# A decoder layer on one core: the setup reordered, constants and selecting columns moved

## The reference

```python
xx = shift(x, 1 token) - x                      # attention with decay, 32 heads of 8
r, k, v, g = (x + xx * maa_*) @ W*.T + b*;  g = silu(g)
w = exp(-exp(time_decay));  u = time_faaaa
Wm = where(i > j, w ** (i - j - 1), where(i == j, u, 0))     # per head
y = (r @ k * Wm) @ v + (state of earlier chunks)
y = (group_norm(y, 8 per head) * ln_g + ln_b) * g @ Wo.T + bo
# cross attention: 16 heads of 16, causal softmax over 128 keys from the context
# mixture: softmax router, 2 of 8 experts of width 176, a shared one of width 704 with a gate
```

## Time and profile before

| | |
|---|---|
| time, median of 3 | 620.1 us (619.21 to 621.57) |
| profiled execution | 619.4 us, span 617.7 us |
| TensorE busy | 591.4 us of the span (96%), 6488 instructions |
| VectorE, ScalarE, GpSimd busy | 404.3, 279.4, 335.0 us |
| TensorE's mean granted clock | 0.997 |
| setup: first instruction to first scores | 30.8 us |

### The profile page before, as it was taken

How to read it: one execution, slowest core, us unless ns; L and a number is a source line. 1 busy time by engine, 2 the same in 40 slices (tenths; PEclk the granted TensorE clock), 3 DMA queues, 4 the chain that set the end, 5 groups by cost and what they waited for, 6 DMA issues and landing times.

```text
span 617.7 us, 15901 instructions
## 1 busy us (share of the span) xinstructions
PE 591.4 (96%) x6488; PEld 479.7 (78%) x6488; DVE 404.3 (65%) x841; ACT 279.4 (45%) x637; POOL 335.0 (54%) x451
## 2 busy tenths in 40 slices
PE   7997898999999999999999999999999999999997
PEld 6544555645889999755889999864798999899997
DVE  5997896899745666879654666869762565752221
ACT  3876243222336566342335666251435656343332
POOL 7567110337446667614455766515364666619776
PEclk8999999999999999999999999999999999999999
DMA  8941000001121121011121112002021112115320
GB/s 192 341 128 36 0 2 2 2 19 54 37 77 35 46 65 45 14 29 59 28 84 30 43 55 59 21 18 71 14 54 38 41 45 61 31 52 126 88 56 18
DMA packets 41906, 34.18 MB, mean 55 GB/s; under 512 B 9917, under 2 KB 41286, under 8 KB 41834
## 3 DMA queue, kind: packets, MB, share of 16 engines
q1 hardware_dynamic: 39930, 31.34, 18.7%
q10 hardware_dynamic: 1904, 1.84, 0.9%
HBM read 30.98 MB, written 2.17 MB: 54 GB/s over the span
## 4 chain that ended last, share of the span: by engine, by line
PE 62%; DVE 19%; POOL 6%; issue 6%; ACT 5%; DMA 1%; ACTq 0%; POOLq 0%; DVEq 0%
DVE A L1630 8%; PE bank L1071 8%; PE bank L1072 7%; PE bank L1073 7%; PE bank L1067 7%; PE bank L1110 4%; PE bank L1111 4%; PE bank L1269 4%; PE bank L1113 3%; PE bank L1196 2%; PE bank L1064 2%; POOL hb L646 2%; PE bank L1350 2%; PE bank L1183 2%; PE bank L1320 2%
## 5 line engine op out<-in xcount | busy, mean ns | idle before, releaser
L633 POOL TENSOR_TENSOR hT<-hb,hT 128x256 fp32r<-128x256 f32 (+1 forms) x102 | 78.3, 768 | 71.7 <-ACT hT L816 71.7
L646 POOL TENSOR_TENSOR hb<-hb,cwb 128x256 f32<-128x256 f32 (+1 forms) x102 | 76.9, 754 | 53.3 <-DVE hb L1605 52.9
L1605 DVE TENSOR_TENSOR hb<-hb,bank 128x256 f32<-128x256 f32 (+1 forms) x102 | 42.7, 418 | 95.7 <-ACT hb L826 95.7
L816 ACT ACTIVATE hT<-hb 128x256 fp32r<-128x256 f32 (+1 forms) x102 | 42.4, 416 | 119.2 <-POOL hb L646 112.0
L1071 PE MATMUL bank<-xTf,wGh 128*128 128x256 f32 x272 | 82.5, 303 | 0.0
L1630 DVE TENSOR_TENSOR A<-bank,decay 128x512 f32<-128x512 f32 x128 | 77.3, 682 | 3.9 <-PE bank L1183 3.8
L1073 PE MATMUL bank<-xTf,wGl 128*128 128x256 f32 x272 | 75.9, 279 | 0.0
L1072 PE MATMUL bank<-xTf,wGh 128*128 128x256 f32 x272 | 75.9, 279 | 0.0
L1072 PE MATMUL bank<-xTf,wUh 128*128 128x256 f32 x256 | 71.5, 279 | 0.0
L1071 PE MATMUL bank<-xTf,wUh 128*128 128x256 f32 x256 | 71.5, 279 | 0.0
L1073 PE MATMUL bank<-xTf,wUl 128*128 128x256 f32 x256 | 71.3, 279 | 0.0
(11 more groups left out here) (235 smaller groups left out, 1405.8 us busy)
## 6 DMA issues: line engine op xcount, KB each, us to landing
cwb<-cw_rows SPq DMA_DIRECT2D x54, 128.0 KB, 2.9
A<-cw_rows SPq DMA_DIRECT2D x18, 128.0 KB, 4.0
A<-in_x SPq DMA_DIRECT2D x4, 512.0 KB, 4.4
res<-in_x SPq DMA_DIRECT2D x4, 512.0 KB, 4.3
out_x<-res SPq DMA_DIRECT2D x8, 256.0 KB, 2.7
rawG<-in_L_ffn_w_gate SPq DMA_DIRECT2D x2, 704.0 KB, 6.4
rawU<-in_L_ffn_w_up SPq DMA_DIRECT2D x2, 704.0 KB, 6.8
cwb<-cw_rows SPq DMA_DIRECT2D x12, 112.0 KB, 2.6
```

The costliest lines, as they stand in the source:

```text
L633: pool.tensor_tensor(low, hb[hr, c % 2, :], hT[hr, c % 2, 0, :].bitcast(F32), ALU.subtract).then_inc(h_lo, 1)
L646: pool.tensor_tensor(hb[hr, c % 2, :], hb[hr, c % 2, :], cwb[hr, c % CWS, :], ALU.mult).then_inc(h_scaled, 1)
L816: act.activation(hT[hidden(n), c % 2, 0, :], hb[hidden(n), c % 2, :], ACT.Copy).then_inc(h_hi, 1)
L1605: tt(h, h, up_part(PS[5 + c % 2], n), ALU.mult).then_inc(gu_used, 1)
```

## The change

Setup: VectorE takes the statistics of x ahead of `td_neg`. TensorE turns the norm ahead of the fourth weight, with no idle products ahead of it, and issues three idle products instead of five behind the weights. ScalarE takes the fourth weight after the first half of the turned norm, and `W_OUT` after r. Of the low 16 heads, VectorE adds the diagonal of the first eight; for heads 8 to 15 ScalarE writes diagonal matrices (`low_bonus_part`, eight instructions around the key copies) and GpSimd adds them at once (`low_diagonal`). `headsel` is written in two halves, one behind the second mixed input, one behind the eighth receptance, and `rev` behind that. The additions of the high diagonal come one receptance later.

Group 0: the seven score banks have another order, and the waits go with it (the gate is waited for by score product 6 in place of 3). `selecting_columns` moves behind `layer_rstd(1, g)`. Three of the four masking products of `key_scores` move into `turn_maxima`, in place of three idle products. `layer_apply(0, 1)` moves ahead of `attended(0)`.

```diff
         W_EARLY = 4
-        SCORE_BANKS = [0, 1, 3, 2, 5, 6, 7]
+
+        def score_bank(g, n):
+
+            return ([0, 1, 3, 2, 5, 6, 7] if g else [0, 1, 3, 5, 6, 7, 2])[n % 7]
...
                 made(pool.memset(onesp[:, w, XD * w:XD * w + XD], 1.0))
-            for n in range(E):
-                made(pool.memset(rev[:, n:n + 1], float(E - n)))
...
-            for b in range(GB):
+            def heads_of(b):
                 rows = headsel[32 * b:32 * b + 32]
...
                                             pattern=[[sign * P, KC], [sign, P]], channel_multiplier=-sign * N))
-            assert done[0] == CONSTS, done[0]
+
+            pool.wait_ge(xm_ready, 2)
+            heads_of(0)
+            heads_of(1)
...
+            def low_diagonal():
+                hs = slice(H // 4, H // 2)
+                pool.wait_ge(decay_cut, 1)
+                pool.wait_ge(low_bonus_made, 1)
+                pool.tensor_tensor(decay[:, hs, :], decay[:, hs, :], bonus[:, hs, :], ALU.add).then_inc(decay_half, 1)
+
             decay_cut_half(0)
...
             receptance(0, 1)
+            low_diagonal()
             decay_cut_half(1)
...
                         split_down(u)
-                    if g == 0 and u == 2:
+                    if g == 0 and u == 3:
                         diagonal(0)
-                    elif g == 0 and u == 3:
+                    elif g == 0 and u == 4:
                         diagonal(1)
...
                 if g == 0:
+                    pool.wait_ge(rbd_ready, 8)
+                    heads_of(2)
+                    heads_of(3)
+                    for n in range(E):
+                        made(pool.memset(rev[:, n:n + 1], float(E - n)))
+                    assert done[0] == CONSTS, done[0]
                     for n in range(3):
...
                     pool.wait_ge(xvp_rest, 2)
-                    selecting_columns()
                 point(g, "n1")
...
                 layer_rstd(1, g)
+                if g == 0:
+                    selecting_columns()
                 point(g, "n3")
...
-            def take_rk(g, key):
+            def take_rk(g, key, parts=range(2)):
                 if g == 0 and not key:
...
                     act.activation(rT[:, m, :], PS[r_bank(g, m)][:, :], ACT.Identity, bias=cols[:, BR, m:m + 1]).then_inc(r_ready, 1)
-                for m in range(2) if key else ():
+                for m in parts if key else ():
                     act.wait_ge(proj_done, g * 8 + 2 + m + 1)
...
             def bonus_half(n):
-                if n == 0:
-                    act.wait_ge(row_in, 16 * 8)
+                if n == 1:
+                    act.wait_ge(decay_half, 1)
                 for h in range(n * H // 4, (n + 1) * H // 4):
...
+            def low_bonus_part(n):
+                for h in range(n * H // 8, (n + 1) * H // 8):
+                    last = act.activation(bonus[:, h, :], ident[:], ACT.Copy, scale=tf[:, h:h + 1])
+                if n == 3:
+                    last.then_inc(low_bonus_made, 1)
+
             mixed_input(0)
+            take_weight(3, wA[:, 3])
             take_weight(W_O, wO[:])
             take_weight(W_Q, wQh[:])
-            take_weight(W_OUT, wX[:])
             decay_powers(0)
             take_rk(0, 0)
-            take_rk(0, 1)
+            take_weight(W_OUT, wX[:])
+            low_bonus_part(2)
+            take_rk(0, 1, (0,))
+            low_bonus_part(3)
+            take_rk(0, 1, (1,))
             decay_powers(1)
...
             idle_product(8, 7, True)
-            for n in range(W_EARLY):
+            for n in range(W_EARLY - 1):
                 turn_weight(n)
-            idle_product(5, 7, True)
             turn_norm(0, 0, tokx, 2)
-            for n in range(W_EARLY, W_KV):
+            for n in range(W_EARLY - 1, W_KV):
                 turn_weight(n)
-            idle_product(5, 4, True)
+            idle_product(3, 4, True)
             project(0, 0)
...
                     m, t = u // 4, slice((u % 4) * T, (u % 4 + 1) * T)
-                    if u == 0:
-                        if g == 0:
-                            pe.wait_ge(w_taken, taken_by_act(8))
+                    if u == 0 and g == 0:
+                        pe.wait_ge(w_taken, taken_by_act(W_OUT))
                     if u == 0 or u == 4:
...
                             pe.wait_ge(v_ready, g * 2 + 2)
-                        elif n == 3 and g != 1:
+                        elif n == 3 and g >= 2:
                             pe.wait_ge(g_ready, g * 2 + 2)
+                        elif n == 4 and g == 0:
+                            pe.wait_ge(w_taken, taken_by_act(W_KV))
+                        elif n == 5 and g == 0:
+                            pe.wait_ge(w_taken, taken_by_act(W_RT))
+                        elif n == 6 and g == 0:
+                            pe.wait_ge(g_ready, 2)
                         elif n == 4 and g >= 2:
...
                         rows = slice(32 * i, 32 * i + 32)
-                        mm(PS[SCORE_BANKS[n % 7]][:, :], kT[rows, m, t], rbd[rows, u % 2, :, :], start=True, stop=True).then_inc(s_ready, 1)
+                        mm(PS[score_bank(g, n)][:, :], kT[rows, m, t], rbd[rows, u % 2, :, :], start=True, stop=True).then_inc(s_ready, 1)
...
+                def later_queries_only(bank):
+                    mm(PS[bank][:, :], maskS[:], identb[:].unsqueeze(1).to_broadcast([P, 4, P]), start=True, stop=False, skip_group_check=True)
+
                 def turn_maxima(b):
...
                         pe.wait_ge(max_ready, b + 1)
-                        idle_product(3, score_base(g, b) + 1)
+                        for i in (1, 2, 3):
+                            later_queries_only(score_base(g, b) + i)
                     pe.wait_ge(nm_ready, g * 4 + b + 1)
...
-                def later_queries_only(bank):
-                    mm(PS[bank][:, :], maskS[:], identb[:].unsqueeze(1).to_broadcast([P, 4, P]), start=True, stop=False, skip_group_check=True)
-
                 def key_scores(b):
                     t = slice(b * T, (b + 1) * T)
-                    if g == 0:
-                        for i in (1, 2, 3):
-                            later_queries_only(score_base(g, b) + i)
                     pe.wait_ge(nmT_ready, g * 4 + b + 1)
...
             nc.vector.tensor_reduce(xcol[:], mcol[:].rearrange("p (w j) -> p w j", w=2), AX, ALU.add).then_inc(mask_cols, 1)
+            dve.wait_ge(x_in, 16)
+            layer_stats(0, 0, tokx)
             dve.wait_ge(td_exp, 1)
             ts(td, td, 1.0e30, -1.0, ALU.min, ALU.mult).then_inc(td_neg, 1)
-            dve.wait_ge(x_in, 16)
-            layer_stats(0, 0, tokx)
             dve.wait_ge(bias_in, 16)
...
             take_v(0, (1,))
-            low_bonus(4, H // 2)
+            low_bonus(4, H // 4)
...
                     first = 16 * (u // 4) + 4 * i
-                    if g == 0 and i == 0 and u % 4 == 0:
-                        dve.wait_ge(*((decay_low, H // 2) if u == 0 else (decay_high, 2)))
+                    if g == 0 and u == 0 and i % 2 == 0:
+                        dve.wait_ge(*((decay_half, 1) if i else (decay_low, H // 4)))
+                    elif g == 0 and u == 4 and i % 2 == 0:
+                        dve.wait_ge(decay_high, i // 2 + 1)
                     if u == 1 and i == 2 and g:
...
                     tt(att[:, (u % 2) * 4 + i, :].rearrange("p (j t) -> p j t", j=4),
-                       PS[SCORE_BANKS[(4 * u + i) % 7]][:, :].rearrange("p (j t) -> p j t", j=4),
+                       PS[score_bank(g, 4 * u + i)][:, :].rearrange("p (j t) -> p j t", j=4),
                        decay[:, first:first + 4, :], ALU.mult).then_inc(pt_ready, 1)
...
                     point(g, "x0a")
+                    layer_apply(0, 1, tokx, tokx)
                     attended(0)
-                    layer_apply(0, 1, tokx, tokx)
                     attended(1)
```

More of the change, by code:

```diff
@@ L221, in decoder_layer @@
         decay_low = sem("decay_low")
+        decay_half = sem("decay_half")
+        low_bonus_made = sem("low_bonus_made")
         decay_high = sem("decay_high")
@@ L767, in _ @@
             take_weight(1, wA[:, 1])
-            take_weight(3, wA[:, 3])
             def mixed_input(g):
```

## The result

The changed kernel takes 624.18 us (median of 7, 623.11 to 626.42) against 620.25 (median of 7): a ratio of 1.0058, 95% interval 1.0033 to 1.0083, thus slower by about 3.6 us by this ratio of mean times; the medians differ by 3.9. The profiled execution has a span of 621.7 us and a time of 623.4; 4.0 us more span than before. The forecast was 623.9, with 0.48 for slower. TensorE's mean granted clock differs between executions of one kernel (0.992 to 0.997 over the seven of the changed one), so that a profile shows one course of several.

What follows compares the result with a forecast made beforehand. TensorE, busy from 120 us on, passes any earlier shift whole to the end. Terms +1.2 + 0.35 + 3.05 - 0.15 - 0.6 = +3.85, on the median of 620.1, gave 623.9 us; range 618.0 to 626.5.

Steps and rivals of the forecast that it cites:

- What bounds: From 120 us on TensorE is busy without slack, so a shift there reaches the end whole.
- Setup, -0.2: Up to the first scores: a norm 1.5 us earlier reaches them as only 0.15 to 0.4; taken as -0.2 us.
- Group norm, +1.0 to +1.4: GpSimd's later residual addition collides with VectorE's root steps: +1.0 to +1.4 us with setup's -0.2 inside, taken as +1.2.
- selecting_columns, +0.35 and +3.05: Behind layer_rstd(1): normalisations beside it +0.35 us; last three selections take turns with VectorE's splits, TensorE starts 3.05 us later.
- the sign I had named: Sign of being right: TensorE's first query scores wait about 3 us for GpSimd.
- Maxima and norm of group 1, -0.6: Moved masks and earlier layer_apply(0, 1) together save 0.6 us by the projections of group 1; bounds 0 and -1.0.
- 1: Rival: selections finish ahead of VectorE's splits and cost nothing; +0.8 us, 620.9, chance 0.15.
- 2: Rival: engines hardly disturb each other at root steps and splits; -1.65 us, 618.5, chance 0.10.
- 3: Rival: earlier norm passes to the scores (-1.85 us) and nothing collides; -3.65 us, 616.5, chance 0.10.
- 4, the clock: Rival: TensorE's clock drops behind a wait before the query scores, or stays low in setup; +1.2 us, 625.1, chance 0.20.
- one of my signs of being wrong: Sign against the forecast: a granted TensorE clock of 0.5 anywhere after 12 us.
- second form of rival 4: In setup, without the removed idle products, norm and four weights are turned at the low clock: +1.2 us, 625.1.

Runs made afterwards that it cites:

- e6: Kernel before plus only the three masks in place of idle products and layer_apply(0, 1) ahead of attended(0): ratio 1.0001, 619.41 us.
- e9: Kernel before, with only group 0's residual addition and selecting_columns moved behind the 13th root step: ratio 0.9988, 618.72 us.
- e2: Changed kernel with headsel's last two quarters and rev written behind the third receptance instead of the eighth: ratio 1.0047, 622.47 us.
- e5: Changed kernel with group 0's residual addition moved behind the 13 root steps, the memsets ahead of it: ratio 1.0050, 623.31 us.
- e8: Changed kernel with headsel's rest and rev behind the third receptance, residual addition and selecting_columns behind root step 13: ratios 0.9970 and 0.9973, 617.67 and 617.87 us.
- e4: Changed kernel with VectorE's three splits moved behind the statistics of group 1, selecting_columns left behind layer_rstd(1): ratio 1.0136, 628.16 us.
- e10: e2 with TensorE's wait for the 14 fences moved from ahead of query_scores(0) to ahead of key_scores(0): ratio 1.0009, 620.54 us.
- e7: Changed kernel with eight more idle products on TensorE behind the turned second norm of group 0: ratio 1.0069, 623.80 us.
- e1: Changed kernel with selecting_columns back behind the two memsets that follow the residual addition: ratio 1.0042, 622.35 us.
- e3: Changed kernel with the edits of e1 and e2 together: ratio 1.0002, 620.03 us.

## Why the prediction was right, and where not

**What bounds.** A shift at the first maxima reached the end: +3.86 there, +4.0 in the span.

**Setup, -0.2.** Most steps went as told: statistics at 5.64 (5.75 forecast), norm turned at 11.24 (11.45), projections at 14.25 (14.15), gate at 30.9 (31.4). The second half of v was added at 28.39, not 31.45, so that the gate and not v held the scores. In the taking of turns I had put the second half of v 3.1 us too late. The profile shows -0.6 at the first root step, but that compares an execution at full clock in setup with one at 1.2 GHz from 8 to 11: the old setup in e6, at full clock, reached it at 54.72 too. At like clock the new setup brings 0 to 0.5 (see e9), timed about 0.9 with an interval of 0.3 to 1.4.

**Group norm, +1.0 to +1.4.** The chain became 1.38 us longer and ended at 61.63 (61.85 or 62.25 forecast). e2 and e5 show the cause: step 3 takes 0.97 or 0.60 as soon as the residual addition is elsewhere, and e8, with the memsets gone too, 0.23. One detail was wrong: I let step 3 in behind the addition and made step 4 wait for the memsets. Step 3 waited for the addition and both memsets, 3.04 us in one piece.

**selecting_columns, +0.35 and +3.05.** The second normalisation took 1.89 instead of 1.38 (+0.51). Three selections took turns with three splits, as forecast; the last fence fell 9.1 us behind the root (9.4 forecast). From the end of the normalisation to the first maxima it is 9.42 us, before 7.05: +2.4, against 3.05 less 0.15. e4 (splits away: 2.6 us, all selections 0.20) shows that the splits are what held the selections, e10 (the wait away) that the wait for them is what cost. But the sign I had named, a wait of TensorE of about 3 us for GpSimd, did not come: it waited 0.88, since the query projection ran at the low clock and ended at 80.3, 0.9 us ahead of the last fence; in e7, at the full clock, it ended 2.14 us ahead of it. I had each of the two as a cause for itself, and they overlapped. Here the Trainium skill's rule ("SBUF — State Buffer", Who interferes with whom), under which the second operation waits for the whole of the first, agrees with the trace: 1.64, 1.40 and 1.39 us behind splits of 1.6.

**Maxima and norm of group 1, -0.6.** Wrong: the trace has 24.15 us against 24.17, and e6 24.13. The masks went, but the copy of the turned maxima on ScalarE stands behind the exponentials there (turned at 105.26, copied at 105.64 to 105.92), and the last mask waits for it; before, the masks had covered just that time. The first attended block came later, as told, and the second was the bound as before.

**The sum.** In the profile: -0.6 at the first root step, +1.4 root steps, +0.2 between them and the second norm, +0.5 normalisation, +2.4 to the maxima, 0.0 after: +3.9. My terms were -0.2, +1.4, 0, +0.35, +2.9 and -0.6. That the totals agree within 0.1 us is luck: the missing 0.6, and 0.35 between the root steps and the end of the normalisation, were made up by 0.4 in setup, which is the clock of that execution, and 0.5 at the maxima. The mechanism of the two large terms was right: collisions with the root steps and with the splits. The low clock, which I had only as a rival, has a part in the second.

**The rivals.** 1 and 2 (fences ahead of the splits; hardly any disturbance) are out by the timelines. 3 (the earlier norm passes to the scores without any collision) is out by the same timelines; of its 1.85 for setup, profiles at like clock show 0 to 0.5. 4, the clock, happened but not as priced. It is also one of my signs of being wrong (a granted clock of 0.5 after 12) that did come. In the changed kernel it is low at 62 to 66, behind the 2.80 us wait for the root steps, where it cost 0.2 us by e7, and at 76 to 79, under the wait for the fences, where it adds nothing to them but by e4 would have held the scores until 80.3 without them. It is why single repairs give so little: e1 has it behind a wait of 3.49, e2 and e5 behind one of 2.43, e7 behind one of 2.14, and each time it cost about 1.5 us. In the profiled executions of e3 and e8, where TensorE's longest waits there are 1.4 us, it does not fall between 45 and 90 us. The length of a wait alone does not decide it: behind the same 2.80 us it fell in the changed kernel and in e4, not in e7, and at 541 us it fell behind 1.2 and 0.4 us in e10, not in e3. What does decide was not tested.

The second form of rival 4 (transposes alone do not bring the clock back in setup) is out. In the changed kernel's execution the norm and four weights, transposes only, were followed by six idle products and the projections, and the granted clock did not fall there. In e3 it was low from 8 us and came back by 11.5, while TensorE did only transposes until 13.00. The rule that I had weighed, by which transposes do not bring the full clock (the Trainium skill, "TensorE: Matmul & The Clock Gate", Part 4), does not agree with this: 0.50 at 10 to 11 and 1.00 at 11.5 to 12. Whether the fp32 transposes of this kernel are of the form that the page means, the profile does not show.

## What to carry to other kernels

Before work of GpSimd is moved "into a gap", look at what VectorE does in the new place from SBUF to SBUF: a short chain of GpSimd operations beside three splits became 3.8 us longer, while beside products from PSUM nothing of the kind was seen (GpSimd's 128x1024 additions to the decay table took 2.37 and 2.38 us there, and 2.80 beside VectorE's mixed inputs). Put it where VectorE reads PSUM or where nobody waits for either (e8). And when several stalls bring the same engine to rest, repair them together before judging one: alone they showed about a quarter of their worth, since TensorE's clock fell at the next one. Before two executions are compared, look whether their granted clocks fell in the same places: one such stretch far from the edit was worth 1.7 us.

## What the runs showed of the hardware that was not expected

A VectorE `tensor_scalar` from SBUF to SBUF did not take its turn: it waited through three GpSimd operations in a row (residual addition and two memsets, 3.04 us) and through two memsets in a row (0.95 to 0.99 in five kernels). `scalar_tensor_tensor` and `tensor_tensor` did take turns with GpSimd's selections, one for one: 19.7 in setup, and the splits at 76 to 81 us. Why the one waits and the others take turns was not tested.

TensorE's clock went from 1.2 back to 2.4 GHz while it did only transposes (e3, 11.5 us), and behind like waits it fell in one execution and not in another (2.80 us: the changed kernel and e7; 1.2 and 0.4 us: e10 and e3).
